# Keys and queries, values and local attention: sorted planes for LN1, and alternating column blocks

## The chip, the cores and the metric

The kernel runs on 1 core of a Trainium2 chip. The metric is the device time in microseconds (us), the median of the runs; lower is better. The core has TensorE (PE; its weight loads are shown apart as PEld), VectorE (DVE), ScalarE (ACT), GpSimd (POOL) and SyncE (SP, which only issues DMAs here). Everything is float32 apart from two constant matrices.

## The reference

Input `x` has shape (8, 32, 32, 32): 8 images, 32 channels, 32 x 32 pixels. Two layers follow each other.

```python
def layer0(x):                                  # 8 heads, d = 4 channels a head
    xn = ln_last(x, ln1_g, ln1_b)               # over the 32 columns of a row
    q, k, v = [conv(conv(xn, w1, 0), w3, 1).reshape(B, 8, H * W, 4) for w1, w3 in qkv]
    probs = softmax(einsum('bhpd,bhpe->bhde', k, q) / scale)
    attn = einsum('bhpd,bhde->bhpe', v, probs).transpose(0, 1, 3, 2).reshape(B, C, H, W)
    x = conv(attn, o_w, 0) + x
    xn = ln_last(x, ln2_g, ln2_b)
    return conv(gelu(conv(conv(xn, g1), g3)) * conv(conv(xn, i1), i3), r1) + x

def layer1(x):
    out = leaky_relu(instance_norm(conv(x, conv1_w, 1)))
    out1, mask = conv(out, conv2_w, 1), sigmoid(conv(out, mask_w, 1))
    xm = out * mask                             # q, k, v: 1x1 convolutions of xm
    out2 = attention of each pixel over its 3 x 3 neighbourhood
    return x + out1 * mask + (1 - mask) * out2
```

The reshape to (heads, H*W, 4) in `layer0` is of memory as it lies: a channel's image is cut into runs of 4 consecutive pixels, so the four entries of a head's vector are the columns x mod 4 = 0, 1, 2, 3 of one channel.

## The kernel before

The 8 images are worked in 4 pairs. A tensor of a pair stands as [128 partitions, 2 images, 256]: partition 32 r + c is channel c of row block r (8 rows of 32 pixels). For a 3 x 3 convolution the kernel builds shifted copies ("planes"): `sh_ln1` has 128 partitions, four blocks of 32 channels, and block s holds the whole image (34 rows with the padding) shifted by s - 1 columns, so that one matmul contracts over channels and columns at once and only the three rows dy are summed in PSUM. `shift_copies` (line 273) makes them out of `ln1_out`, cut by row blocks: DVE copies block 3 and block 0 (8 copies), ACT half of block 1 and block 2 (6 copies), and SP the other half of block 1 with two DMAs (`ln1_planes`, line 316). The same helper makes the planes of LN2, x2 and `act_c`; all DVE copies stand under line 278, all ACT copies under line 467.

Where the planes of LN1 are read:
- `qk` (line 1132): for each image, half, two column offsets d and three dy, one matmul with `sh_ln1` as stationary operand. Its 128 columns are 128 pixels with x mod 4 = d, taken with a step of 4 elements. The moving operand is the weight `w_qk`, 128 columns. 24 matmuls a pair.
- `v_by_head` (line 1143): 12 matmuls a pair, `w_v` (32 columns) stationary, the moving operand 512 pixels of the planes with a step of 4; output d goes to the PSUM partitions 32 d to 32 d + 31, which is column block d of the array.

`ln_apply` (lines 733 and 737) ends a layer norm: a product and a subtraction on DVE, 128 x 512 each. In local attention `window_scores` (line 1278) has, for each of two banks, 16 matmuls with a stationary operand of 64 columns, first 8 for column block 0 and then 8 for block 64; `window_out` (line 1302) has 32 matmuls with 32 stationary and 64 moving columns, 8 for each of four column blocks, block by block. A float32 matmul is two passes in the trace, so its counts are twice these.

The order on each engine is written out by hand, with semaphores between them. First comes the front of pairs 0 and 1, then a loop body `step(pair)`, run for pair 0 and (without the layer norm of a further pair) for pair 1, then a tail for pairs 2 and 3. In a body TensorE does the second layer of pair p, q/k and v of pair p + 2 between `conv1` and `mask_conv` of pair p, and the gate of pair p + 1 after the window scores. DVE's part for LN1 of pair p + 3 stands between `window_probs(p)` and `gated(p + 1)`. `average_mean` (line 1209) is a small matmul in the middle of `qk` that waits for DVE's statistics of `conv1`.

## Time and profile before

| | us |
|---|---|
| runs: median of 3 (lowest, highest) | 289.95 (288.15, 292.16) |
| profiled execution: span from its first to its last instruction | 286.2 |
| PE busy | 222.9 (78%) |
| PE weight loads busy | 143.5 (50%) |
| DVE busy | 189.8 (66%) |
| ACT busy | 129.2 (45%) |
| POOL busy | 75.9 (27%) |

The profiled execution is given by its span; some microseconds of a run lie outside it. Engines work side by side, so shares do not add up. Start and duration are in microseconds from the start of the span; "idle before" is the time for which an engine had nothing to do before a group, with the engine, tile and line that ended it. Names are those of the program with buffer numbers left out: `sh_ln` is `sh_ln1` or `sh_ln2`, `ln_out` is `ln1_out` or `ln2_out`.

### The profile page before, as it was taken

How to read it: one execution, taken by the hardware profiler on the slowest of the kernel's cores; microseconds unless marked ns; L12 is line 12 of the kernel's file. 1: busy time of each engine (PE TensorE's matmuls, PEld its weight loads, DVE VectorE, ACT ScalarE, POOL GpSimd, SP SyncE). 2: the span in 40 equal slices, each digit the busy share in tenths (PEclk: the TensorE clock that was granted, in tenths of full speed). 3: DMA queues.
4: the chain of work that ended last, by engine and by line, in shares of the span. 5: the costliest groups of instructions: out<-in, count | busy, mean ns of one | idle time of the engine just before them, and what ended most of it. 6: DMA issues, size and time to landing. Idle time of an engine off the chain costs nothing.

```text
span 286.2 us, 4575 instructions
## 1 busy us (share of the span) xinstructions
PE 222.9 (78%) x1738; PEld 143.5 (50%) x1738; DVE 189.8 (66%) x417; ACT 129.2 (45%) x256; POOL 75.9 (27%) x56
## 2 busy tenths in 40 slices
PE   0429868999669997798999986998529989368963
PEld 0229518824229734654589255745115536136843
DVE  5595365527596768999747974835999738882532
ACT  2230142234383355549822565429347557444440
POOL 3928204004004302540045125000464300304150
PEclk9999997999979999799999997999859999779987
DMA  7210011000011000000000200000000000000101
GB/s 198 53 46 2 0 40 53 0 2 0 1 55 37 2 0 1 2 0 21 0 2 0 73 3 1 2 0 2 0 37 3 0 0 3 0 0 3 39 0 39
DMA packets 3654, 5.17 MB, mean 18 GB/s; under 512 B 1136, under 2 KB 1872, under 8 KB 3632
## 3 DMA queue, kind: packets, MB, share of 16 engines
q1 hardware_dynamic: 3392, 4.29, 5.0%
q10 hardware_dynamic: 240, 0.58, 0.6%
q8 instruction: 14, 0.23, 0.3%
q14 instruction: 8, 0.07, 0.1%
HBM read 3.30 MB, written 1.05 MB: 15 GB/s over the span
## 4 chain that ended last, share of the span: by engine, by line
PE 64%; DVE 17%; ACT 10%; issue 5%; DMA 2%; SPq 0%; ACTq 0%; DVEq 0%
PE ps L1132 16%; PE ps L1186 15%; PE ps L1143 8%; PE ps L1278 6%; PE ps L1302 5%; PE ps L1222 4%; ACT sh_ln L467 4%; ACT p_t L560 3%; DVE sh_in L278 3%; DVE sh_ln L278 2%; DMA w3b<-in_w_gi 2%; PE ps L1262 2%; PE ps L1112 2%; DVE q_bd L933 1%; DVE xm L922 1%
## 5 line engine op out<-in xcount | busy, mean ns | idle before, releaser
L1132 PE MATMUL ps<-w_qk,sh_ln 128*128 128x128 f32 x192 | 46.9, 409 | 11.6 <-DVE sh_ln L278 7.8
L376 POOL TENSOR_TENSOR ln_s<-ln_s,neg_half 128x16 f32<-128x16 f32 x8 | 23.3, 2910 | 112.6 <-DVE ln_s L726 112.6
L1132 PEld LDWEIGHTS ps<-w_qk,sh_ln 128*128 128x128 f32 x192 | 45.6, 330 | 14.3 <-issue 14.3
L1186 PE MATMUL ps<-sh_ln,w_gi 96*128 96x512 f32 x96 | 42.4, 596 | 0.5 <-ACT v L484 0.5
L1222 PE MATMUL ps<-sh_in,w_in 128*32 128x256 f32 x384 | 25.6, 424 | 10.6 <-DVE sh_in L278 10.6
L467 ACT ACTIVATE sh_ln<-ln_out 32x496 f32<-32x496 f32 (+1 forms) x44 | 27.2, 618 | 11.6 <-DVE ln_out L737 11.0
L278 DVE COPY sh_ln<-ln_out 32x496 f32<-32x496 f32 (+2 forms) x60 | 28.0, 466 | 3.4 <-PE ps L1143 2.4
L1186 PEld LDWEIGHTS ps<-sh_ln,w_gi 96*128 96x128 f32 x96 | 17.9, 190 | 22.1 <-issue 21.9
L1222 PEld LDWEIGHTS ps<-sh_in,w_in 128*32 128x32 f32 x384 | 13.3, 123 | 23.3 <-DVE sh_in L278 10.8
L1143 PE MATMUL ps<-sh_ln,w_v 128*32 128x512 f32 x96 | 22.4, 1077 | 0.0
L829 DVE TENSOR_TENSOR gi<-ps,gate 64x512 f32<-64x512 f32 x16 | 11.1, 694 | 13.9 <-ACT gate L498 13.5
L479 ACT ACTIVATE qk_t<-ps 128x512 f32<-128x512 f32 x8 | 4.8, 597 | 34.0 <-PE ps L1132 34.0
L498 ACT ACTIVATE gate<-ps 64x512 f32<-64x512 f32 x16 | 9.4, 587 | 22.1 <-PE ps L1186 22.1
L1302 PE MATMUL ps<-p_t,v_t 128*32 128x64 f32 x256 | 14.2, 235 | 5.5 <-ACT p_t L560 5.5
L1278 PE MATMUL ps<-k_h,q_bd 128*64 128x60 f32 x256 | 17.8, 245 | 0.0
L1278 PEld LDWEIGHTS ps<-k_h,q_bd 128*64 128x64 f32 x256 | 16.6, 158 | 2.0 <-issue 2.0
L278 DVE COPY sh_in<-act_c 32x496 f32<-32x496 f32 (+1 forms) x28 | 17.2, 614 | 0.5
L1302 PEld LDWEIGHTS ps<-p_t,v_t 128*32 128x32 f32 x256 | 13.6, 120 | 7.7 <-issue 7.7
L1112 PE MATMUL ps<-sh_x,w_conv 128*32 128x512 f32 x96 | 12.4, 656 | 3.0 <-DVE sh_x L278 3.0
L467 ACT ACTIVATE sh_in<-act_c 32x496 f32<-32x496 f32 (+1 forms) x20 | 12.3, 617 | 4.9 <-DVE act_c L894 4.7
L400 POOL TENSOR_TENSOR omm<-ones,msk 128x512 f32<-128x512 f32 x4 | 6.6, 1648 | 28.2 <-DVE msk L912 28.0
L467 ACT ACTIVATE sh_x<-x 32x496 f32<-32x496 f32 (+1 forms) x20 | 12.3, 616 | 3.8 <-DVE x L836 3.6
(125 smaller groups left out, 336.5 us busy)
## 6 DMA issues: line engine op xcount, KB each, us to landing
x_norm<-in_x SPq DMA_DIRECT2D x4, 256.0 KB, 2.8
x_res<-in_x SPq DMA_DIRECT2D x4, 256.0 KB, 2.5
out_x<-out_s SPq DMA_DIRECT2D x4, 256.0 KB, 2.0
sh_ln<-ln_out SPq DMA_DIRECT2D x8, 64.0 KB, 2.0
kc<-in_shape_consts ACTq DMA_DIRECT2D x1, 450.0 KB, 5.8
w3b<-in_w_gi SPq DMA_DIRECT2D x1, 288.0 KB, 6.3
vec<-in_vectors SPq DMA_DIRECT2D x1, 131.5 KB, 3.3
w3a<-in_w_qkv ACTq DMA_DIRECT2D x1, 108.0 KB, 3.3
```

The lines of the kernel that those rows point to most:

```text
L278: ins = copy(plane(planes)[C * s:C * s + C, :, 1 + RH * r:1 + RH * r + RH, cut_left:cut_left + n], src[C * r:C * r + C, :, :].rearrange("p ...
L376: nc.gpsimd.tensor_tensor(ln_s[n][:, 3, :], ln_s[n][:, 2, :], neg_half[:, :], ALU.pow)\
L467: return nc.scalar.activation(o, i, ACT.Copy)
L498: nc.scalar.activation(gate[EC:P, n, :], ps[0:EC, GI_BANKS[n], :], ACT.Gelu).then_inc(g_gelu.sem, 1)
L829: nc.vector.tensor_tensor(gi[EC * (n % 2):EC * (n % 2) + EC, n // 2, :], ps[EC:P, GI_BANKS[n], :], gate[EC:P, n, :], ALU.mult).then_inc(g_ ...
L1112: mm = nc.tensor.matmul(ps[C * r:C * r + C, bank, :], weight(dy), plane(planes)[:, :, RH * r + dy:RH * r + dy + RH, 0:W], start=(dy == 0), ...
L1132: mm = nc.tensor.matmul(to, sh_ln1[:, i, at:at + D * P - D + 1:D], w_qk[:, dy, :, :, :].rearrange("p d m c -> p (d m c)"), start=(dy == 0) ...
L1143: mm = nc.tensor.matmul(ps[C * d:C * d + C, 2, :], w_v[:, dy, :], xs[:, :, dy:dy + H, d:d + W - D + 1:D], start=(dy == 0), stop=(dy == 2))
L1186: mm = nc.tensor.matmul(ps[:, GI_BANKS[2 * i + h], :], w_gi[:, dy, :, :].rearrange("p m o -> p (m o)"), xs[:, i, y:y + H // 2, 0:W], start ...
L1222: mm = nc.tensor.matmul(ps[C * r:C * r + C, bank, BLK * i:BLK * i + BLK], w_in[:, i, k, dy, :], plane(sh_in)[:, i, RH * r + dy:RH * r + dy ...
L1278: mm = nc.tensor.matmul(ps[C * r:C * r + 2 * C, 5 + bank, KEYS * n:KEYS * n + KEYS], q_bd[:, u, r:r + 2, :].rearrange("p r m -> p (r m)"), ...
L1302: mm = nc.tensor.matmul(o[:, i, a, b:b + 2, :, :], v_t[:, t, C * r:C * r + C], p_t[:, R * t + r, :, :].rearrange("p h m -> p (h m)"), star ...
```

## The change

`ln1_out` gets the form [128, 7 slots, 2 images, 8 rows x 8]. Slot 1 + d holds the pixels with x mod 4 = d; slot 0 holds those one column to the left of offset 0 (offset 3 of the neighbour at left), slots 5 and 6 those one and two to the right of offset 3. The final subtraction of LN1 writes slots 1 to 4 in that order, reading both operands with a step of 4; `ln1_neighbours`, two new DVE copies, fills slots 0, 5 and 6 from them (the edge stays zero, from a new memset at the start). Block s of `sh_ln1` is then slots s to s + 3 as they are, [4, 2 images, 34 rows x 8], and `slot_copies` takes the place of `shift_copies` for LN1, with the same number of copies on the same engines. `qk` and `v_by_head` read runs of consecutive elements. In `window_scores` and `window_out` the loops are exchanged, so that successive matmuls go to different column blocks. The matmuls and their number stay.

```diff
--- before.py
+++ after.py
@@ -61,6 +61,11 @@
 
 V_BC1, V_BC2, V_BM, V_BQ, V_BK, V_BV, V_SCALE, V_LN, V_OW = 0, 1, 2, 3, 4, 5, 6, 7, 7 + 4 * W
 V_END = V_OW + D * C
+WD = W // D
+SLOTS = D + 3
 
 
 
@@ -131,12 +136,12 @@
         x1 = sb("x1", [P, 2, BLK])
         x2 = sb("x2", [P, 2, BLK])
         out_s = sb("out_s", [P, 2, BLK])
-        ln1_out = sb("ln1_out", [P, 2, BLK])
+        ln1_out = sb("ln1_out", [P, SLOTS, 2, RH * WD])
         ln2_out = sb("ln2_out", [P, 2, BLK])
         act_c = sb("act_c", [P, 2, BLK])
         act_in = sb("act_in", [P, 2, BLK])
         w_in = sb("w_in", [P, 2, 2, 3, C])
-        sh_ln1 = sb("sh_ln1", [P, 2, PLANE])
+        sh_ln1 = sb("sh_ln1", [P, D, 2, (H + 2) * WD])
         sh_ln2 = sb("sh_ln2", [3 * C, 2, PLANE])
         sh_x2 = sb("sh_x2", [P, 2, PLANE])
         sh_in = sb("sh_in", [P, 2, PLANE])
@@ -184,7 +189,7 @@
 
         g_xn = signal("x_for_norm_loaded", 16)
         g_x = signal("x_for_sum_loaded", 16)
-        g_ln = [signal("ln1_steps", 7), signal("ln2_steps", 7)]
+        g_ln = [signal("ln1_steps", 9), signal("ln2_steps", 7)]
         g_sq = [signal("ln1_squares", 1), signal("ln2_squares", 1)]
         g_rs = [signal("ln1_rstd", 1), signal("ln2_rstd", 1)]
 
@@ -280,6 +285,19 @@
                            [:, :, :, cut_right:cut_right + n])
             return ins
 
+        def slot_planes(s, r):
+            at = (1 + RH * r) * WD
+            return sh_ln1[C * s:C * s + C, :, :, at:at + RH * WD].rearrange("p d i m -> p (d i) m")
+        def slots_of(s, r):
+            return ln1_out[C * r:C * r + C, s:s + D, :, :].rearrange("p d i m -> p (d i) m")
+        def slot_copies(copy, s, row_blocks):
+            for r in row_blocks:
+                ins = copy(slot_planes(s, r), slots_of(s, r))
+            return ins
 
         Z_LN1, Z_LN2, Z_X2, Z_IN, Z_PADS = 3, 4, 5, 6, 7
         W_QKV, W_ALL = 3, 8
@@ -312,9 +330,7 @@
                 sp.wait_ge(g_v4.sem, g_v4.before(pair))
                 sp.wait_ge(g_ln[0].sem, g_ln[0].done(pair))
                 for r in range(R // 2):
-                    start = (1 + RH * r) * W
-                    sp.dma_start(sh_ln1[C:2 * C, :, start:start + BLK], ln1_out[C * r:C * r + C])\
-                      .then_inc(planes_by["ln1"]["dma"].sem, 16)
+                    sp.dma_start(slot_planes(1, r), slots_of(1, r)).then_inc(planes_by["ln1"]["dma"].sem, 16)
 
             def store(pair):
                 alone(sp)
@@ -470,8 +486,12 @@
 
                 act.wait_ge(src_ready.sem, src_ready.done(pair))
                 act.wait_ge(reader.sem, reader.before(pair))
-                shift_copies(act_copy, src, dst, 1, range(R // 2, R) if name == "ln1" else (R - 1,))
-                shift_copies(act_copy, src, dst, 2, range(R)).then_inc(planes_by[name]["act"].sem, 1)
+                if name == "ln1":
+                    slot_copies(act_copy, 1, range(R // 2, R))
+                    slot_copies(act_copy, 2, range(R)).then_inc(planes_by[name]["act"].sem, 1)
+                else:
+                    shift_copies(act_copy, src, dst, 1, (R - 1,))
+                    shift_copies(act_copy, src, dst, 2, range(R)).then_inc(planes_by[name]["act"].sem, 1)
 
             def qk_t_evac(pair, i):
                 act.wait_ge(g_qkt.sem, g_qkt.at(pair, i + 1))
@@ -671,6 +691,7 @@
         def _(dve):
             for t in (w_bd, w_r1, w_conv, ps[:, 0, 0:12 * C], ps[:, 2, 0:3 * C]):
                 nc.vector.memset(t[:], 0.0).then_inc(s_zero_bd, 1)
+            nc.vector.memset(ln1_out[:, :, :, :], 0.0).then_inc(s_zero_bd, 1)
             dve.wait_ge(s_vec, 16)
 
             def folded_qkv():
@@ -734,8 +755,22 @@
                   .then_inc(g.sem, 1)
                 dve.wait_ge(g.sem, g.at(pair, 6))
                 planes_read(name, pair)
-                nc.vector.tensor_tensor(dst[:, :, :].rearrange("p i (y x) -> p (i y) x", x=W),
-                                        ln_per_col(2 * n + 1), ln_d[n][:, :, :], ALU.subtract).then_inc(g.sem, 1)
+                by_col, centered = ln_per_col(2 * n + 1), ln_d[n][:, :, :]
+                if n == 0:
+                    to = dst[:, 1:1 + D, :, :].rearrange("p d i (y x) -> p d (i y) x", x=WD)
+                    by_col, centered = [t.rearrange("p y (x d) -> p d y x", d=D) for t in (by_col, centered)]
+                else:
+                    to = dst[:, :, :].rearrange("p i (y x) -> p (i y) x", x=W)
+                nc.vector.tensor_tensor(to, by_col, centered, ALU.subtract).then_inc(g.sem, 1)
+            def ln1_neighbours(pair):
+                g = g_ln[0]
+                dve.wait_ge(g.sem, g.at(pair, 7))
+                rows = ln1_out[:, :, :, :].rearrange("p d i (y x) -> p d (i y) x", x=WD)
+                nc.vector.tensor_copy(rows[:, 0, :, 1:WD], rows[:, D, :, 0:WD - 1]).then_inc(g.sem, 1)
+                nc.vector.tensor_copy(rows[:, D + 1:SLOTS, :, 0:WD - 1], rows[:, 1:SLOTS - D, :, 1:WD])\
+                  .then_inc(g.sem, 1)
 
             def planes_read(name, pair):
 
@@ -748,10 +783,11 @@
                 dve.wait_ge(src_ready.sem, src_ready.done(pair))
                 dve.wait_ge(reader.sem, reader.before(pair))
                 if name == "ln1":
-                    shift_copies(nc.vector.tensor_copy, src, dst, 3, range(R))
+                    slot_copies(nc.vector.tensor_copy, 3, range(R))
+                    slot_copies(nc.vector.tensor_copy, 0, range(R)).then_inc(planes_by[name]["dve"].sem, 1)
                 else:
                     shift_copies(nc.vector.tensor_copy, src, dst, 1, range(R - 1))
-                shift_copies(nc.vector.tensor_copy, src, dst, 0, range(R)).then_inc(planes_by[name]["dve"].sem, 1)
+                    shift_copies(nc.vector.tensor_copy, src, dst, 0, range(R)).then_inc(planes_by[name]["dve"].sem, 1)
 
             def ln1_center(pair):
                 dve.wait_ge(g_xn.sem, g_xn.done(pair))
@@ -759,6 +795,7 @@
 
             def ln1_apply(pair):
                 ln_apply(0, ln1_out, "ln1", pair)
+                ln1_neighbours(pair)
                 planes("ln1", ln1_out, sh_ln1, g_ln[0], g_v4, pair)
 
             sm3 = [sm[:, k, :].rearrange("p (i e) -> p i e", e=D) for k in range(3)]
@@ -1017,6 +1054,7 @@
 
             ln1_center(0)
             ln_var(0, 0)
+            dve.wait_ge(s_zero_bd, 6)
             folded_qkv()
             dve.wait_ge(s_zero, Z_LN1)
             ln1_apply(0)
@@ -1025,6 +1063,7 @@
             other_constants()
             clear(ps[:, 4, :], ps[:, 7, :])
             ln_apply(0, ln1_out, "ln1", 1)
+            ln1_neighbours(1)
             head_scores(0)
             head_max(0)
             head_mix(0)
@@ -1128,8 +1167,8 @@
                         to = ps[:, i, 2 * P * h:2 * P * h + 2 * P]\
                             .rearrange("p (m d c) -> p d m c", m=2, d=D)[:, d:d + 2, :, :]
                         for dy in range(3):
-                            at = W * (H // 2 * h + dy) + d
-                            mm = nc.tensor.matmul(to, sh_ln1[:, i, at:at + D * P - D + 1:D],
+                            y = H // 2 * h + dy
+                            mm = nc.tensor.matmul(to, sh_ln1[:, d, i, WD * y:WD * y + P],
                                                   w_qk[:, dy, :, :, :].rearrange("p d m c -> p (d m c)"),
                                                   start=(dy == 0), stop=(dy == 2), skip_group_check=True)
                 if 1 in halves:
@@ -1137,11 +1176,10 @@
 
             def v_by_head(pair):
 
-                xs = plane(sh_ln1)
                 for dy in range(3):
                     for d in range(D):
                         mm = nc.tensor.matmul(ps[C * d:C * d + C, 2, :], w_v[:, dy, :],
-                                              xs[:, :, dy:dy + H, d:d + W - D + 1:D],
+                                              sh_ln1[:, d, :, WD * dy:WD * dy + WD * H],
                                               start=(dy == 0), stop=(dy == 2))
                 mm.then_inc(g_v4.sem, 1)
 
@@ -1271,10 +1309,10 @@
 
                     nc.tensor.matmul(ps[:, 5 + bank, 0:UPB * KEYS], ident_bf[:, :], win_bf[:, :],
                                      start=True, stop=False, skip_group_check=True)
-                    for r in range(0, R, 2):
-                        for n in range(UPB):
-                            u = UPB * bank + n
-                            i, a, b = u // (TA * TB), u // TB % TA, u % TB
+                    for n in range(UPB):
+                        u = UPB * bank + n
+                        i, a, b = u // (TA * TB), u // TB % TA, u % TB
+                        for r in range(0, R, 2):
                             mm = nc.tensor.matmul(ps[C * r:C * r + 2 * C, 5 + bank, KEYS * n:KEYS * n + KEYS],
                                                   q_bd[:, u, r:r + 2, :].rearrange("p r m -> p (r m)"),
                                                   k_h[:, i, TH * a:TH * a + KH, TW * b:TW * b + KW],
@@ -1295,10 +1333,10 @@
             def window_out(pair):
                 alone(pe)
                 pe.wait_ge(g_t_sb.sem, g_t_sb.done(pair))
-                for r in range(R):
-                    o = ps[C * r:C * r + C, 5, :].rearrange("p (i a y b x) -> p i a b y x", i=2, a=TA, b=TB, x=TW)
-                    for t in range(UNITS // 2):
-                        i, a, b = t // (TA * TB // 2), t // (TB // 2) % TA, 2 * (t % (TB // 2))
+                for t in range(UNITS // 2):
+                    i, a, b = t // (TA * TB // 2), t // (TB // 2) % TA, 2 * (t % (TB // 2))
+                    for r in range(R):
+                        o = ps[C * r:C * r + C, 5, :].rearrange("p (i a y b x) -> p i a b y x", i=2, a=TA, b=TB, x=TW)
                         mm = nc.tensor.matmul(o[:, i, a, b:b + 2, :, :], v_t[:, t, C * r:C * r + C],
                                               p_t[:, R * t + r, :, :].rearrange("p h m -> p (h m)"),
                                               start=True, stop=True)
```

On DVE the place is LN1 of pair p + 3 in the loop body, between the window softmax (`wsm`, `prob`) and the gating (`gi`), before:

```order
L967 TENSOR_TENSOR prob<-prob,wsm 128x8x60
L733 TENSOR_TENSOR ln_d<-ln_d,ln_s 128x512
L737 TENSOR_TENSOR ln_out<-vec,ln_d 128x512
L278 COPY sh_ln<-ln_out 32x2x8x30 x4
L278 COPY sh_ln<-ln_out 32x2x8x31 x4
L829 TENSOR_TENSOR gi<-ps,gate 64x512 x4
```

and now:

```order
L1004 TENSOR_TENSOR prob<-prob,wsm 128x8x60
L754 TENSOR_TENSOR ln_d<-ln_d,ln_s 128x512
L764 TENSOR_TENSOR ln_out<-vec,ln_d 128x512
L771 COPY ln_out<-ln_out 128x16x7
L772 COPY ln_out<-ln_out 128x32x7
L298 COPY sh_ln<-ln_out 32x8x64 x8
L866 TENSOR_TENSOR gi<-ps,gate 64x512 x4
```

Two copies stand between the subtraction and the eight copies to the planes, and the latter have runs of 64 elements where they had runs of 30 or 31.

On ACT it is the same place, between the first and second half of the gelu (`gate`), before:

```order
L498 ACT_TABLE_LOAD
L498 ACTIVATE gate<-ps 64x512 x2
L467 ACTIVATE sh_ln<-ln_out 32x2x256 x2
L467 ACTIVATE sh_ln<-ln_out 32x2x8x31 x4
L498 ACTIVATE gate<-ps 64x512 x2
```

and now:

```order
L518 ACT_TABLE_LOAD
L518 ACTIVATE gate<-ps 64x512 x2
L483 ACTIVATE sh_ln<-ln_out 32x8x64 x6
L518 ACTIVATE gate<-ps 64x512 x2
```

Nothing moved; six copies stay six, of 512 elements each. On SP the two DMAs of a pair have pieces of 64 elements instead of 256.

## Rows read from the trace of the kernel before

**Rows 1.** The page: span; busy us, share and instructions by engine.

```profile
span 286.2 us, 4575 instructions
PE 222.9 (78%) x1738; PEld 143.5 (50%) x1738; DVE 189.8 (66%) x417; ACT 129.2 (45%) x256; POOL 75.9 (27%) x56
```

**Rows 2.** The page: the chain that ended last, by line.

```profile
PE ps L1132 16%; PE ps L1186 15%; PE ps L1143 8%; PE ps L1278 6%; PE ps L1302 5%; PE ps L1222 4%; ACT sh_ln L467 4%; ACT p_t L560 3%; DVE sh_in L278 3%; DVE sh_ln L278 2%; DMA w3b<-in_w_gi 2%; PE ps L1262 2%; PE ps L1112 2%; DVE q_bd L933 1%; DVE xm L922 1%
```

**Rows 3.** Timeline, TensorE: start, duration, line, operation, tiles, shapes, count.

```profile
85.37 5.70 PEld L1132 LDWEIGHTS ps<-w_qk,sh_ln 128*128 128x128 f32 x24 [1.94 <-issue]
133.92 0.80 PEld L1289 LDWEIGHTS ps<-kc,prob 128*128 128x128 f32 x7 [0.29 <-issue]
...
98.66 5.59 PE L1143 MATMUL ps<-sh_ln,w_v 128*32 128x512 f32 x24
141.46 2.78 PE L1112 MATMUL ps<-sh_x,w_conv 128*32 128x512 f32 x24
```

**Rows 4.** Stretches: busy PE, PEld, DVE, ACT, POOL; granted clock; DMA.

```profile
45.40:48.70 3.30, 3.30 (x16) 3.30 (x16) 1.26 (x3) 0.36 (x1) 1.93 (x1) 0.50 0.11 42
...
175.20:178.40 3.20, 3.20 (x34) 3.09 (x33) 0.00 (x0) 1.10 (x8) 2.66 (x3) 0.50 0.00 0
```

**Rows 5.** Chain in order of time: start, duration, work.

```profile
235.30 1.82 PE ps L1278 x32
175.22 3.23 PE ps L1278 x32
257.58 3.15 PE ps L1302 x64
277.20 4.71 PE ps L1302 x64
```

**Rows 6.** Groups, 19.6 to 24.8, then 25 to 31: busy us, mean ns.

```profile
L1132 PE MATMUL ps<-w_qk,sh_ln 128*128 128x128 f32 x22 | 5.5, 445 | 7.8 <-DVE sh_ln L278 7.8
L1132 PE MATMUL ps<-w_qk,sh_ln 128*128 128x128 f32 x27 | 6.4, 396 | 0.0
```

**Rows 7.** Timeline, TensorE, values of local attention.

```profile
121.67 1.91 PE L1262 MATMUL ps<-w_bd,xw 128*60 128x128 f32 x30
```

**Rows 8.** Timeline, LN1 of pair 2 and the first `average_mean`.

```profile
81.49 3.77 ACT L467 ACTIVATE sh_ln<-ln_out 32x512 f32<-32x512 f32 x6 [1.32 <-DVE ln_out L737]
...
81.53 1.24 SPq L316 DMA_DIRECT2D sh_ln<-ln_out  x2
...
89.58 0.17 DVE L853 TENSOR_SCALAR inorm_v<-st 128x2 f32<-128x2 f32 x1
91.10 0.28 PE L1209 MATMUL ps<-st,kc 128*128 128x2 f32 x2
```

**Rows 9.** Groups, DVE: a reduction with a step, and one in order.

```profile
L805 DVE TENSOR_REDUCE mix_s<-mix_p 128x64 f32<-128x256 f32 x4 | 2.4, 598 | 0.1
...
L777 DVE TENSOR_REDUCE sc_d<-sc_m 128x8 f32<-128x256 f32 x4 | 1.7, 420 | 0.1
```

**Rows 10.** Timeline, LN1 of pair 0 beside POOL's last memset.

```profile
12.57 6.79 DVE L278 COPY sh_ln<-ln_out 32x480 f32<-32x480 f32 x8
...
14.25 1.91 POOL L370 MEMSET sh_in<- 128x2176 f32 x1
```

**Rows 11.** Timeline, DVE, LN1 of pair 3 and the gating.

```profile
129.56 3.34 DVE L278 COPY sh_ln<-ln_out 32x480 f32<-32x480 f32 x8
...
132.93 2.87 DVE L829 TENSOR_TENSOR gi<-ps,gate 64x512 f32<-64x512 f32 x4
```

**Rows 12.** DMA issues: tiles, queue, count, KB each, median us to landing.

```profile
sh_ln<-ln_out SPq DMA_DIRECT2D x8, 64.0 KB, 2.0
...
w_bd<-in_l_qkv SPq DMA_DIRECT2D x4, 12.0 KB, 3.5
```

**Rows 13.** Timeline, ACT's planes of LN2, DVE's of `act_c`.

```profile
104.93 3.13 ACT L467 ACTIVATE sh_ln<-ln_out 32x512 f32<-32x512 f32 x5
...
154.09 5.40 DVE L278 COPY sh_in<-act_c 32x512 f32<-32x512 f32 x7
```

## The prediction, made before the changed kernel had run

> **What bounds the kernel now.** I read the page's engine shares first: PE is busy 78% of a span of 286.2 us [rows 1]. Then the chain that ended last: its largest lines are PE's L1132 (q/k, 16%), L1186 (15%) and L1143 (v, 8%); L1278 (window scores) and L1302 (window output) have 6% and 5% [rows 2]. So TensorE sets most of the end, and the change touches four of these five lines. Next the timeline, for what one instruction costs. A float32 matmul stands in the trace as two passes, each a weight load (PEld) and a MATMUL. In q/k the 24 weight loads of one image take 5.70 us, 0.238 each, back to back: the stationary operand is `sh_ln1` read at every fourth element. The transposes L1289 load as many columns from consecutive elements, 7 in 0.80 us, 0.114 each. In v the moving operand is strided: 24 passes take 5.59 us, while L1112, with the same shapes (128x32 stationary, 512 columns) and rows read in order, takes 2.78 [rows 3]. Both strided reads cost twice the contiguous one, on either operand, and this is the sentence on which most of the forecast rests.
>
> **Part 1, q/k.** 48 passes a pair, each 0.238 -> 0.114: 5.9 us a pair, 23.7 for the four. Bounds: nothing (if the loads are slow for another reason) and 23.7. Here the clock comes in. While loads took 0.238 a lower clock was hidden: from 45.4 to 48.7 the granted clock was 0.50 (1.2 GHz) and q/k kept its pace, 16 passes in 3.3 us with those that overlap the ends [rows 4]. Once a pass is short the matmul shows it: 32 score passes take 3.23 us at half clock and 1.82 at full [rows 4, 5], a factor 1.77, so a q/k pass costs 0.20 there. The second pair has 3.4 us of it (loss 1.5 us). For the first pair the view of the clock shows nothing of the kind, but its MATMULs average 445 ns up to 24.8 and 396 after [rows 6]; I take the first 5.2 us to be at half clock too: 26 passes where full clock would give 46, a loss of 2.3. Part 1 is 23.7 - 3.8 = 19.9.
>
> **Part 2, v.** 5.59 - 2.78 = 2.8 a pair, 11.2 in all.
>
> **Part 3, alternating column blocks.** How much two blocks overlap is seen in L1262, where successive matmuls already alternate between two: 30 passes with 128 moving columns in 1.91 us, 0.064 each [rows 7], against 0.114 in L1289 [rows 3]. So I halve the scores: a bank's 32 passes 1.82 -> 0.95. For window output (four blocks, 64 passes, 3.15 us [rows 5]) the ends are nothing and a quarter (0.8); I take 1.8, since no row shows weight loads this close together with so few moving columns, and two blocks are the nearest. At half clock, the last one, 4.71 us [rows 5] also goes to about 1.8.
>
> **Part 4, what is added.** On DVE a memset of 896 elements, before `vec` lands, where DVE has nothing: nothing. Per pair: two neighbour copies of 112 and 224 elements, and the subtraction at the old L737 reads both operands and writes at a step. The copies: 0.2 and 0.3 us, between the row of a copy of about 500 elements (3.34/8 = 0.42, [rows 11]) and nothing. The subtraction: a reduction of 256 elements takes 0.60 us with a step and 0.42 in order [rows 9]; twice that difference for 512 is 0.35. Together 0.9 us, ends 0.3 and 1.5. (The Trainium skill, SBUF — State Buffer, Specifications, gives SBUF lines of 16 bytes and wants two hits on each for full bandwidth; a step of four floats gives one. By that rule the subtraction would double, to 1.4 us instead of 1.04, and the sum lose about 1 us more, 261; the reductions of [rows 9] show a factor of 1.4, the matmuls one of 2.) The slot copies are as many and as long as the shift copies: nothing. All copies to `sh_ln1` (DVE 8, ACT 6, two DMAs) now wait for the neighbours.
> - Pair 0: DVE's first shift copy is held until POOL's memset ends at 16.16 (8 copies take 6.79 us), while ACT and the DMAs ran beside it [rows 10]. The neighbour copies will be held there instead, and ACT's six copies (3.77) start only behind them, at about 16.6: q/k starts 0.9 us later.
> - Pair 2: PE waits for ACT's copies in 81.49 to 85.27 [rows 8]: 0.9 later.
> - Pair 3: the planes are done long before their use. But DVE runs without a pause there until the gating [rows 11]: 0.9 later on `gi`, less 0.5 because the second score bank no longer keeps DVE waiting.
> - DMA pieces shrink from 1024 to 256 bytes. Issued at 81.53, the second one lands 1.24 + 2.0 = 3.2 us later, ACT takes 3.77 [rows 8, 12]. The nearest row for small pieces is `w_bd` (128 bytes, from HBM) at 3.5 us: then the planes are 1.0 late in three pairs. I take 0, with 3 us as the other end.
>
> **Where gains get lost.** In iteration 0 DVE's statistics are ready at 89.75; PE asks at 91.1 [rows 8]. PE will ask 2.9 us sooner than before relative to its start, DVE 0.9 later than ACT's copies allow: 1.5 us of waiting. After v, ACT copies ln2's planes (3.13 us) before it can do the tanh [rows 13]; ACT now gets ahead of DVE's `ln2_out`, 1.1 us lost. In iteration 1 DVE's seven `in` copies take 5.40 us, since POOL's final operations hold them [rows 13]; before, q/k and v covered them; now they end 1.2 after v, and ln2's planes behind them hold the tanh 1.6 longer. Small hand-offs around v4: 0.2.
>
> **Sum.** 19.9 + 11.2 = 31.1. Less 0.9, 0.9, 1.5, 1.1, 2.8, 0.2: 23.7. Pair 0's second half +0.5 (scores 0.5, output 0.9, DVE -0.9), pair 1: scores 1.3, output 1.1. That makes 26.6. Pair 2's scores lie beside DVE's copies of x2 (0.2), its output is on the chain (1.3); pair 3's scores give 1.4, its output 2.9: 5.8. Total 32.4. Shorter bursts leave PE more pauses, and half clock came only after pauses; a stretch of 3.4 us does 1.9 us' worth of work, so costs 1.5 where PE is the bound. I allow one and a half new ones, 2.4. Gain 30.0. The profiled span is 286.2; the median of the runs is 289.95, so 3.7 us lie outside it and stay: 286.2 - 30.0 + 3.7 = **260.0 us**.
>
> **Rivals.**
> - A, the hand-offs or the clock eat more (0.16): four new half-clock stretches (6 us), or DVE and ACT the bound after each q/k, so that a third of Part 1 is lost: 265 to 272. For: PE's waits are already on DVE and ACT. Against: PE's own lines stand on top of the chain [rows 2].
> - B, the weight loads are not slow for their step (0.07): the output of q/k is written in runs of 32 floats, and w_qk may matter. Then the 19.9 of Part 1 is gone, and with it some 3 of the lost hand-offs and 2 of the clock: 32.4 - 19.9 + 3 = 15.5, about 275. Against: v shows the same factor.
> - C, the DMA copies end last (0.04 by itself): q/k of three pairs starts up to 1 us later, 263. The Trainium skill (DMA: Bandwidth & Descriptors, Specifications) wants at least 512 bytes for line rate and so speaks against 256-byte pieces; the same page calls slow small descriptors a matter of HBM only. By the first the time would be that 263.
> - D, better (0.08): window output at a quarter (1.0 less three times) and no new half clock (2.4): 254.6 or a little less.
> - E, slower (0.02): TensorE sinks to 1.2 GHz for good. Each 3.4 us stretch costs 1.5, so it decides from 21 new stretches on (32.4 / 1.5), 71 us more at half clock; if all of the 150 us of PE that remain on the chain ran there, x 1.77, it would be some 375 us. Against: the scores that took 3.23 at 175 take 1.82 at 235 [rows 5], so it comes back.
> - F, hardly any change (0.03): behind PE's savings DVE and ACT set each iteration, and only the 5.8 us of the last two pairs arrive: 284. Against: in iteration 1 nothing but PE separates the start of q/k from the end of v, save the copies named.
>
> **Range and chances.** The forecast (254 to 265) has 0.60. To hold 8 in 10 I take in half of A and of D, C, and the ends of Part 4: 253 to 269. A measurement of this kernel tells about 2%, 5.8 us, from no change. Faster by over that: forecast, A, B, C, D, 0.95. Within: F, 0.03. Slower: E, 0.02.
>
> **What would show it.** L1132's successor: 48 loads a pair near 0.114, half-clock stretches excepted. v: 24 passes in about 2.8. Scores 32 passes near 1 us at full clock, output 64 near 1.8. The subtraction near 1.0 us, neighbours 0.2 and 0.3. The mean matmul (average) of iteration 0 waits for DVE's statistics. What would make it wrong: q/k loads still above 0.2; PE waiting for `sh_ln1` by a DMA; a PE clock at 0.5 in most slices; PE idle after v longer than 3 us an iteration.

## The result, and the profile after the change

The changed kernel takes 258.5 us (median of four runs, 254.9 to 260.7) against 289.7 for the kernel before on the same chip: a ratio of 0.885, 95% interval 0.879 to 0.892. The forecast was 260.0, range 253 to 269. A second measurement (e9 below) gave 258.5 again and a ratio of 0.894 (0.889 to 0.898), so two measurements of one kernel differ by about 1%, and smaller differences between the experiments below are told as such. Every ratio and its interval leave out runs more than 1.5% above the fastest of their kernel (the slow ones), while the medians hold all runs.

The page of the changed kernel, first busy time by engine, then the chain by engine and by line. These answer [rows 1, 2].

```profile
span 256.4 us, 4585 instructions
PE 182.8 (71%) x1738; PEld 111.0 (43%) x1738; DVE 192.4 (75%) x426; ACT 129.3 (50%) x256; POOL 76.1 (30%) x56
...
DVE 43%; PE 36%; ACT 8%; issue 7%; DMA 3%; POOL 1%; SPq 1%; ACTq 0%; DVEq 0%
PE ps L1224 12%; DVE sh_in L283 6%; PE ps L1171 5%; PE ps L1260 5%; DVE sh_ln L298 3%; DVE sh_ln L283 3%; DMA w3b<-in_w_gi 3%; ACT sh_x L483 2%; PE ps L1151 2%; DVE ln_out L764 2%; PE ps L1232 2%; DVE sh_x L283 2%; PE ps L1316 2%; PE ps L1300 2%; DVE gi L866 2%
```

TensorE lost 40 us of busy time and DVE gained 2.6. q/k (old L1132, now L1171) fell from 16% of the chain to 5%; v (old L1143, now L1181), with 8% before, is not among its lines any more. DVE, with 43% of the chain, now sets more of the end than TensorE. The next matmul to look at is not one of these any more, it is the gate/info convolution, L1224.

The four groups that the change is about. Each row: line, engine, operation, tiles, shapes, count, busy us, mean ns of one, idle time before. Before, the same groups stood at 46.9 (L1132), 22.4 (L1143), 17.8 (L1278) and 14.2 us (L1302).

```profile
L1171 PE MATMUL ps<-w_qk,sh_ln 128*128 128x128 f32 x192 | 26.6, 302 | 12.8 <-ACT sh_ln L483 12.8
L1181 PE MATMUL ps<-sh_ln,w_v 128*32 128x512 f32 x96 | 11.1, 596 | 0.0
L1316 PE MATMUL ps<-k_h,q_bd 128*64 128x60 f32 x256 | 10.8, 246 | 0.0
L1340 PE MATMUL ps<-p_t,v_t 128*32 128x64 f32 x256 | 6.9, 290 | 5.1 <-ACT p_t L580 5.1
```

And the price of one pass, from the timeline of TensorE and its weight loads (start, duration, line, operation, tiles, shapes, count). These answer [rows 3] and [rows 5].

```profile
77.92 1.42 PEld L1171 LDWEIGHTS ps<-w_qk,sh_ln 128*128 128x128 f32 x12
82.42 2.78 PE L1181 MATMUL ps<-sh_ln,w_v 128*32 128x512 f32 x24
151.29 1.97 PE L1316 MATMUL ps<-k_h,q_bd 128*64 128x60 f32 x32
210.18 1.15 PE L1316 MATMUL ps<-k_h,q_bd 128*64 128x60 f32 x32
171.99 1.10 PE L1340 MATMUL ps<-p_t,v_t 128*32 128x64 f32 x64 [0.76 <-ACT p_t L580]
232.66 1.94 PE L1340 MATMUL ps<-p_t,v_t 128*32 128x64 f32 x64 [2.25 <-ACT p_t L580]
```

Twelve loads of q/k take 1.42 us, 0.118 each; v's 24 passes 2.78. Scores and window output have two prices each: at full clock 1.15 and 1.10 us, at half clock 1.97 and 1.94. The granted clock of the stretches says which is which (busy time of PE, PEld, DVE, ACT, POOL; granted clock; DMA):

```profile
147.10:157.10 10.00, 8.78 (x86) 6.39 (x88) 6.05 (x13) 4.88 (x21) 3.78 (x3) 0.50 0.01 2
...
232.40:235.60 3.20, 2.94 (x69) 2.81 (x70) 0.17 (x1) 0.80 (x2) 0.18 (x1) 0.50 0.02 5
```

### The profile page after: what moved, and what is told of

The parts are those of the page before. It is cut to its first block, busy times and chain, and to the rows that moved or that the text cites. A ratio compares the mean times of both kernels' runs of the same rounds, so it can differ in the third digit from the quotient of the medians.

```text
span 256.4 us, 4585 instructions
## 1 busy us (share of the span) xinstructions
PE 182.8 (71%) x1738; PEld 111.0 (43%) x1738; DVE 192.4 (75%) x426; ACT 129.3 (50%) x256; POOL 76.1 (30%) x56
## 4 chain that ended last, share of the span: by engine, by line
DVE 43%; PE 36%; ACT 8%; issue 7%; DMA 3%; POOL 1%; SPq 1%; ACTq 0%; DVEq 0%
PE ps L1224 12%; DVE sh_in L283 6%; PE ps L1171 5%; PE ps L1260 5%; DVE sh_ln L298 3%; DVE sh_ln L283 3%; DMA w3b<-in_w_gi 3%; ACT sh_x L483 2%; PE ps L1151 2%; DVE ln_out L764 2%; PE ps L1232 2%; DVE sh_x L283 2%; PE ps L1316 2%; PE ps L1300 2%; DVE gi L866 2%
## 5 line engine op out<-in xcount | busy, mean ns | idle before, releaser
L1224 PE MATMUL ps<-sh_ln,w_gi 96*128 96x512 f32 x96 | 42.4, 596 | 0.5 <-DVE sm L822 0.5
L483 ACT ACTIVATE sh_ln<-ln_out 32x512 f32<-32x512 f32 (+1 forms) x44 | 27.4, 622 | 22.0 <-DVE ln_out L772 15.3
L1171 PE MATMUL ps<-w_qk,sh_ln 128*128 128x128 f32 x192 | 26.6, 302 | 12.8 <-ACT sh_ln L483 12.8
L1260 PE MATMUL ps<-sh_in,w_in 128*32 128x256 f32 x384 | 26.2, 432 | 11.4 <-DVE sh_in L283 11.4
L1171 PEld LDWEIGHTS ps<-w_qk,sh_ln 128*128 128x128 f32 x192 | 25.4, 216 | 16.4 <-issue 16.4
L1224 PEld LDWEIGHTS ps<-sh_ln,w_gi 96*128 96x128 f32 x96 | 17.9, 190 | 22.1 <-issue 21.9
L866 DVE TENSOR_TENSOR gi<-ps,gate 64x512 f32<-64x512 f32 x16 | 11.1, 694 | 15.0 <-ACT gate L518 14.7
L518 ACT ACTIVATE gate<-ps 64x512 f32<-64x512 f32 x16 | 9.3, 587 | 20.2 <-PE ps L1224 20.2
L1151 PE MATMUL ps<-sh_x,w_conv 128*32 128x512 f32 x96 | 12.7, 664 | 5.7 <-DVE sh_x L283 4.4
L298 DVE COPY sh_ln<-ln_out 32x512 f32<-32x512 f32 x32 | 13.4, 418 | 0.5
L283 DVE COPY sh_x<-x 32x496 f32<-32x496 f32 (+1 forms) x28 | 11.5, 411 | 0.5
L283 DVE COPY sh_ln<-ln_out 32x496 f32<-32x496 f32 (+1 forms) x28 | 11.5, 411 | 0.5
L1181 PE MATMUL ps<-sh_ln,w_v 128*32 128x512 f32 x96 | 11.1, 596 | 0.0
L1316 PE MATMUL ps<-k_h,q_bd 128*64 128x60 f32 x256 | 10.8, 246 | 0.0
L398 POOL TENSOR_TENSOR inorm_v<-inorm_v,neg_half 128x2 f32<-128x2 f32 x4 | 4.3, 1076 | 21.9 <-DVE inorm_v L924 21.9
```

What stands on the lines that cost most here:

```text
L283: ins = copy(plane(planes)[C * s:C * s + C, :, 1 + RH * r:1 + RH * r + RH, cut_left:cut_left + n], src[C * r:C * r + C, :, :].rearrange("p ...
L298: ins = copy(slot_planes(s, r), slots_of(s, r))
L483: return nc.scalar.activation(o, i, ACT.Copy)
L518: nc.scalar.activation(gate[EC:P, n, :], ps[0:EC, GI_BANKS[n], :], ACT.Gelu).then_inc(g_gelu.sem, 1)
L866: nc.vector.tensor_tensor(gi[EC * (n % 2):EC * (n % 2) + EC, n // 2, :], ps[EC:P, GI_BANKS[n], :], gate[EC:P, n, :], ALU.mult).then_inc(g_ ...
L1151: mm = nc.tensor.matmul(ps[C * r:C * r + C, bank, :], weight(dy), plane(planes)[:, :, RH * r + dy:RH * r + dy + RH, 0:W], start=(dy == 0), ...
```

## The experiments

The experiments ran on three chips, each beside its own runs of the kernel before: 289.5 us beside e1 to e4, 288.1 beside e5 to e8, 289.1 beside e9 to e12.

**e1 and e2, one half each.** e1 is the kernel before with only the loops of scores and window output exchanged; e2 is the changed kernel with only those loops put back.

```diff
-                    for r in range(0, R, 2):
-                        for n in range(UPB):
-                            u = UPB * bank + n
-                            i, a, b = u // (TA * TB), u // TB % TA, u % TB
+                    for n in range(UPB):
+                        u = UPB * bank + n
+                        i, a, b = u // (TA * TB), u // TB % TA, u % TB
+                        for r in range(0, R, 2):
...
```

> The kernel before with the exchanged loops of window scores and window output alone; the planes of LN1 stay as they were. The theory of the prediction: the score lines fall from 17.8 us of busy time to about 11 and the output from 14.2 to about 7, and on the chain this gives some 9 us (5.8 of them in the last two pairs): about 281 us, ratio 0.97. Rival (the two halves of the change only pay together, or shorter bursts bring more half clock): under 4 us, ratio above 0.985.

> The changed kernel with the loops of window scores and window output in their old order; sorted planes, neighbour copies and reads in order stay. The theory of the prediction: the other 21 to 23 us, about 267 us, ratio 0.925; q/k 26 to 27 us busy, v about 11. If the two halves are worth less together than apart, this kernel and the one with the loops alone gain more than 31 us between them.

e1 took 279.9 us, ratio 0.966 (0.956 to 0.975), e2 266.7, ratio 0.913 (0.904 to 0.923). The gains, 9.6 and 22.8, add up to 32.4 of the whole's 31: the two halves of the change do not help or hinder each other by more than the runs can tell. In e1 the window output of pair 0 (and below it that of pair 2) shows the price of four alternating blocks without the other half:

```profile
137.11 1.10 PE L1302 MATMUL ps<-p_t,v_t 128*32 128x64 f32 x64 [0.58 <-ACT p_t L560]
...
255.55 1.93 PE L1302 MATMUL ps<-p_t,v_t 128*32 128x64 f32 x64 [2.24 <-ACT p_t L560]
```

3.15 became 1.10 at full clock. The output of pair 2 at 255.55 ran at half clock, where the kernel before had full clock for it [rows 5], and so kept only 1.2 of 2.05 us. What e1 changes is the order as a whole: no run changes it and keeps successive matmuls in one block. That the alternation is what pays rests on that order and on the older lines that alternate already [rows 7].

**e3 and e4, is it the step?** e3 is the kernel before, in which each q/k weight load reads 128 consecutive elements of the old plane instead of every fourth (so q and k come from other pixels, as many of them). e4 reads every second element, in q/k and in v (other pixels too).

First the edit of e3, then that of e4.

```diff
-                            mm = nc.tensor.matmul(to, sh_ln1[:, i, at:at + D * P - D + 1:D],
+                            mm = nc.tensor.matmul(to, sh_ln1[:, i, W * (H // 2 * h + dy) + d:W * (H // 2 * h + dy) + d + P],
```

```diff
-                            mm = nc.tensor.matmul(to, sh_ln1[:, i, at:at + D * P - D + 1:D],
+                            mm = nc.tensor.matmul(to, sh_ln1[:, i, at:at + 2 * P - 1:2],
...
-                                              xs[:, :, dy:dy + H, d:d + W - D + 1:D],
+                                              xs[:, :, dy:dy + H, d:d + 15:2],
```

> The kernel before, with only the q/k matmuls reading 128 consecutive elements of the planes instead of every fourth (other pixels, so q and k are not those of the reference); no new copies, v stays strided. Theory (the step makes the weight loads slow): q/k weight loads fall from 45.6 us busy to about 25, and the time by about 16 to 18 us, to 272. Rival B of the prediction (q/k is slow for its scattered output or its moving operand): loads stay near 45 us and the time near 289.

> The kernel before, with q/k and v reading every second element instead of every fourth (other pixels, so q, k and v are not those of the reference). The rule of the Trainium skill (SBUF — State Buffer, Specifications), two hits for each 16-byte line, gives two floats of each line at a step of two: q/k passes at 0.11 us and v's 24 passes in 2.8 us, as if in order. Rival (any step other than one halves the rate): 0.235 and 5.6 as before.

e3 took 271.8 us, ratio 0.943 (0.934 to 0.952), e4 265.7 in its one run. Twelve q/k loads in the kernel before, in e4 and in e3:

```profile
91.21 2.89 PEld L1132 LDWEIGHTS ps<-w_qk,sh_ln 128*128 128x128 f32 x12
```

```profile
79.04 1.50 PEld L1132 LDWEIGHTS ps<-w_qk,sh_ln 128*128 128x128 f32 x12
```

```profile
81.38 1.42 PEld L1132 LDWEIGHTS ps<-w_qk,sh_ln 128*128 128x128 f32 x12
```

0.241 a pass at a step of four floats, 0.125 at two, 0.118 in order. The output is written in the same runs of 32 floats in all three, and `w_qk` is read alike, so rival B, that the loads are slow for something else, falls. And the cost is not "strided or not": a step of two floats costs 6% on the stationary operand. On the moving one it costs more: v's MATMULs take 14.9 us in all in e4, between the 22.4 at a step of four and the 11.1 in order. One pair of it, with the clock at full:

```profile
29.96 3.71 PE L1143 MATMUL ps<-sh_ln,w_v 128*32 128x512 f32 x24
```

The Trainium skill (SBUF — State Buffer, Specifications) wants two hits on each 16-byte line for full bandwidth; a step of two floats gives two hits, a step of four one. The stationary operand follows that within 6%. v at step two is 34% above the row in order, but its reads differ from those in more than the step. They come in runs of 8 elements, a run for each image row, and the runs of d = 2 and 3 start in the middle of a line, so they touch five lines for eight elements and two of the five only once. The single passes in the trace of e4 fall into two kinds, half of them 0.65 us long and half 0.76, where every pass in order takes 0.59. The first two column blocks to start, those of d = 0 and 1 in the kernel's order, have the short ones. So the step itself seems to cost v about 10%, and where its runs start the rest; no run separates the two, and this stays argued.

**e5, the neighbour slots left out.** The changed kernel without the two copies (so slots 0, D + 1 and D + 2 of `ln1_out` stay zero, and the convolution reads zeros there for neighbouring columns; the count of LN1's signals goes from 9 to 7 with them): what do they cost with the wait behind POOL's memset?

```diff
-                nc.vector.tensor_copy(rows[:, 0, :, 1:WD], rows[:, D, :, 0:WD - 1]).then_inc(g.sem, 1)
-                nc.vector.tensor_copy(rows[:, D + 1:SLOTS, :, 0:WD - 1], rows[:, 1:SLOTS - D, :, 1:WD])\
-                  .then_inc(g.sem, 1)
```

> The changed kernel without the two neighbour copies on DVE (slots 0, 5 and 6 keep zeros, so the planes lack their neighbours). By the trace of after, the copies cost 0.5 us a pair where nothing holds them, on the chain in three pairs, and in pair 0 they are held by POOL's memsets until 16.3 while ACT's six copies wait behind them: DVE's own eight copies are held as long, so pair 0 gains only about 0.8. In all 2 to 2.5 us, ratio to the kernel before about 0.877 instead of 0.885. If the copies were worth more than 4 us, the price in Part 4 of the prediction was too low.

255.2 us, ratio 0.885 (0.881 to 0.889), against 0.885 and 0.894 for the changed kernel: between nothing and 1%. The 2 to 2.5 us expected are thus neither shown nor ruled out. The start of pair 0's q/k moves only from 20.41 to 20.00, because the next copies are held in their place:

```profile
13.70 6.01 DVE L298 COPY sh_ln<-ln_out 32x512 f32<-32x512 f32 x8
```

Eight copies that take 3.44 elsewhere take 6.01. So it is not the neighbours that are dear at the start, it is the memset beside them (e6 shows that: without it the neighbours take 0.22 and 0.27 us and the eight copies 3.44).

**e6, POOL's clears behind the second square root.**

```diff
-            clear(sh_ln2)
-            clear(sh_x2)
-            clear(sh_in)
             rstd(0, 1)
+            clear(sh_ln2)
+            clear(sh_x2)
+            clear(sh_in)
```

> The changed kernel with POOL clearing the planes of LN2, x2 and the activation after the second rstd instead of before it. Theory (what holds DVE's copies at 13.4 to 16.4 is POOL's memset, not the data): the neighbour copies take 0.5 us, q/k of pair 0 starts near 17.6 instead of 20.4, and 2.5 to 3 us arrive at the end, about 255.5. Rival: the moved memsets then hold DVE's later copies of pairs 0 and 1, and nothing is gained.

261.4 us, ratio 0.906 (0.903 to 0.910): worse. q/k of pair 0 starts at 17.25, three us earlier, as the theory said. But the clears now stand beside the neighbour copies of pair 1 (first row, DVE), and v of pair 0, queued behind DVE's scores, starts at 33.15 instead of 30.53 and runs at half clock (PE):

```profile
24.66 6.95 DVE L771 COPY ln_out<-ln_out 128x112 f32<-128x112 f32 x1
```

```profile
33.15 5.34 PE L1181 MATMUL ps<-sh_ln,w_v 128*32 128x512 f32 x24
```

A copy of 112 elements, 0.22 us by itself, lasted 6.95 and over the ends of five of POOL's seven memsets; it ended as the last one, of `p_t`, began at 31.49. Three us won at the start were paid for with a hold of seven.

**e7 and e8, filling TensorE's pauses.** In e7 eight matmuls without a use stand ahead of the scores (into a bank that is free there) and four ahead of `reduce_1`; e8 is e6 and e7 together.

```diff
+            def filler(bank, n):
+                for _ in range(n):
+                    nc.tensor.matmul(ps[:, bank, 0:UPB * KEYS], ident_bf[:, :], win_bf[:, :],
+                                     start=True, stop=True, skip_group_check=True)
...
                 window_k(pair)
+                filler(0, 8)
                 window_scores(pair)
...
                 probs_transposed(pair)
+                filler(6, 4)
                 reduce_1(pair + 1)
```

> The changed kernel with matmuls whose results nobody reads in two pauses of TensorE in the loop: 8 of 480 bfloat16 columns ahead of the window scores and 4 ahead of the r1 matmuls. Theory (the pause before the scores brings the stretch of half clock over scores and window v in iteration 1): that stretch goes, the scores' two banks take 1.0 instead of 1.9 us and window v 1.9 instead of 2.6, so 2 to 3 us are gained, and the granted clock rises from 0.90. Rival: the stretches come from low load over a longer time and stay; the fillers then cost up to 1 us.

> The later clears and the filler matmuls together. If both work and lie in different places, their gains add: about 253 us, 5 us under the changed kernel.

e7: 257.7 us, ratio 0.897 (0.892 to 0.903); e8: 261.6, ratio 0.908 (0.903 to 0.913). In e7 the stretch from 147.1 to 157.1, at half clock in the changed kernel, is at full clock (first fence, same columns as above), and the gate/info convolution behind it starts at 155.67 instead of 158.18. But the first convolution of pair 1, 2.78 us in the changed kernel, now meets the half clock (second row of the first fence, and the PE row of the second):

```profile
147.10:157.10 10.00, 8.95 (x114) 6.03 (x115) 7.64 (x18) 6.87 (x24) 3.78 (x3) 1.00 0.01 2
122.40:125.60 3.20, 3.20 (x16) 0.79 (x20) 3.05 (x5) 2.54 (x4) 0.00 (x0) 0.50 0.02 5
```

```profile
122.32 4.42 PE L1151 MATMUL ps<-sh_x,w_conv 128*32 128x512 f32 x24 [1.94 <-DVE sh_x L283]
```

1.6 us are lost there, and at the next q/k e7 is 0.3 behind (126.67 for 126.33); at gate/info it is 2.5 ahead. So the 10 us at half clock had cost 2.8, not the 4.5 that my 1.5 for each 3.4 us gives: TensorE is idle for 1.2 of them anyway. The span of the profiled execution is 1.1 us shorter, the ratio no better. Yet over the whole execution TensorE spent 37 us at half clock instead of 51 (2 x 0.073 x 255.3 us, at a mean granted clock of 0.927, against 2 x 0.100 x 256.4). So 14 us less at half clock shortened the span by 1.1 us, the fillers' own time included. e8 missed its 253 us: it kept e6's loss.

**e9 to e12, a version that avoids e6's fault.** e9 is the changed kernel again, as the reference. e10 puts POOL's clears into gaps and writes the neighbour slots with a two-source operation. e11 is e10 with the one-source copies kept. e12 is e10 with the filler ahead of the scores only. The edit of e10 against the changed kernel:

```diff
             rstd(0, 0)
+            rstd(0, 1)
             clear(sh_ln2)
             clear(sh_x2)
             clear(sh_in)
-            rstd(0, 1)
             clear(xm)
+            rstd(1, 0)
+            rstd(0, 2)
             clear(q_bd, s_late)
             clear(prob, s_late)
             clear(p_t, s_late)
-            rstd(1, 0)
-            rstd(0, 2)
...
-            dve.wait_ge(s_late, 5)
             gated(0, 0)
...
             ln1_apply(2)
+            dve.wait_ge(s_late, 5)
             with dve.Fori(0, PAIRS - 3) as pair:
...
-                nc.vector.tensor_copy(rows[:, 0, :, 1:WD], rows[:, D, :, 0:WD - 1]).then_inc(g.sem, 1)
-                nc.vector.tensor_copy(rows[:, D + 1:SLOTS, :, 0:WD - 1], rows[:, 1:SLOTS - D, :, 1:WD])\
-                  .then_inc(g.sem, 1)
+                for to, x in ((rows[:, 0, :, 1:WD], rows[:, D, :, 0:WD - 1]),
+                              (rows[:, D + 1:SLOTS, :, 0:WD - 1], rows[:, 1:SLOTS - D, :, 1:WD])):
+                    nc.vector.tensor_tensor(to, x, x, ALU.max).then_inc(g.sem, 1)
```

> The changed kernel itself once more, as the reference for the three runs beside it on the same chip. 258.5 us as before, within 1.5 us, and about 0.89 of the kernel before. If it comes out further off, the comparisons of the earlier experiments with it, which were made on other chips, are uncertain by as much.

> Three edits of the start: POOL's clears of the other planes and xm stand behind the second square root, its clears of the window buffers behind the square root of pair 2, and the two copies of the neighbour slots are a maximum of a tensor with itself, which has two sources. Theory (POOL's memset holds one-source copies of DVE and lets two-source operations run): the neighbour slots of pair 1 take 0.2 and 0.3 us beside the memset, where e6 had 6.95, q/k of pair 0 starts at 17.3 us instead of 20.4, planes of pair 1 are at most 1 us late, and 2 to 3 of those 3 us last: 256 us. Rival (DVE is held by POOL's memset whatever the operation is): the maximum is held to the end of the clears, about 29 us, v of pair 0 ends about 2.5 us later than in the changed kernel: 260 us or more. Second rival (what is gained at the start is eaten by another pattern of half-clock stretches): starts moved earlier as in the theory, and the time within 1 us of the changed kernel's.

> The same as e10_start, with the neighbour slots written by one-source copies as in the changed kernel. Theory (one-source copies are held): the copies of pair 1 that start at about 24.7 us end with the memset of xm at about 29 us, 4.3 us after their start, and v of pair 0 ends about 4 us later than in e10_start; 259 us. Rival (length of the hold in e6 had another cause than the kind of operation): same as e10_start.

> e10_start with the eight filler matmuls ahead of the scores of each pair, as in e7, and none ahead of reduce_1. Theory (a pause of TensorE ahead of the scores brings the half clock on scores, v windows and gate/info): the scores of pair 1 take 2.9 us instead of 4.9 wherever they had fallen to half clock, about 1 to 2 us less in the span than e10_start: 254.5 us. Rival (the half clock is only moved to another place, as conv1 of pair 1 showed in e7): within 1 us of e10_start.

| kernel | us, median | ratio, interval |
|---|---|---|
| e9, the changed kernel | 258.5 | 0.894 (0.889 to 0.898) |
| e10 | 256.1 | 0.879 (0.872 to 0.885) |
| e11 | 257.2 | 0.888 (0.883 to 0.893) |
| e12 | 256.6 | 0.886 (0.880 to 0.892) |

e10's ratio goes by its two faster runs, 253.3 and 254.8 us; the other two took 257.3 (the profiled one) and 258.0. All four are below e9's four, 258.2 to 259.0.

The neighbours of pair 1 in e10 (two operations in 0.58 us) and in e11 (3.71 us, to the end of POOL's memset of `sh_in`):

```profile
25.44 0.58 DVE L773 TENSOR_TENSOR ln_out<-ln_out 128x112 f32<-128x112 f32 x2
```

```profile
25.32 3.71 DVE L771 COPY ln_out<-ln_out 128x112 f32<-128x112 f32 x1
...
27.05 1.90 POOL L386 MEMSET sh_in<- 128x2176 f32 x1
```

In both kernels POOL runs the same memsets, from 23.5 to 29.7 us. This shows it: POOL's memset holds DVE's one-source copies and lets its two-source operations run. The Trainium skill (SBUF — State Buffer, SBUF: two separate sides) has the rule: GpSimd and a DVE operation in a two-port mode lock each other out for a whole instruction, and a DVE operation with two SBUF inputs only meets a GpSimd operation that reads SBUF, which a memset does not. The rows agree on both counts; that the hold can outlast a memset and go on through the next ones (one boundary in e11, five in e6) is what the rows add.

What comes of the earlier start: e10 starts q/k at 18.04, where the changed kernel starts it at 20.41 in its first trace and at 20.63 in that of e9. But e10 ends it at 26.42, the changed kernel at 27.78 and, in e9, at 28.61. The loads per 2 us (busy time and count of PEld, granted clock, DMA) show why. For e10, then the first trace of the changed kernel:

```profile
18.00:20.00 2.00, 2.00 (x10) 1.00 0.02 7
...
22.00:24.00 2.00, 2.00 (x11) 1.00 0.00 0
24.00:26.00 2.00, 2.00 (x19) 1.00 0.06 12
```

```profile
20.50:22.50 2.00, 2.00 (x11) 1.00 0.00 0
22.50:24.50 2.00, 2.00 (x13) 1.00 0.00 0
24.50:26.50 2.00, 2.00 (x19) 1.00 0.04 8
```

And for e11, whose q/k starts at 17.91, and for e9:

```profile
20.00:22.00 2.00, 2.00 (x15) 1.00 0.00 0
22.00:24.00 2.00, 2.00 (x20) 1.00 0.03 8
```

```profile
24.50:26.50 2.00, 2.00 (x15) 1.00 0.00 0
26.50:28.50 2.00, 2.00 (x20) 1.00 0.05 12
```

In all of them the loads first come at 0.21 us each. That is the pace of a recorded half clock: from 37.8 to 41.2 in the changed kernel, at 0.50, a q/k load takes 0.213 too. The slow pace ends at 21.0 us in e11, 24.0 in e10, 24.1 in the changed kernel and 25.7 in e9, which is the same kernel. The 1.00 in these rows is no measurement: the trace's own record of the clock begins with an entry of full clock at just these times (21.0, 23.9, 24.1, 25.6), and the view counts time without an entry as full. So the first stretch of q/k ran at half clock, as the prediction took it to; where it ends differs by 1.5 us between two executions of one kernel, and an earlier start can mean more work at the slow pace.

How much of the start lasts can be read against two traces of the changed kernel, and they differ. Against the first, the 1.35 us that e10 is ahead at the first convolution of pair 0 (66.05 for 67.40) are gone at the first `average_mean`, 77.56 for 77.70: q/k of pair 2 meets half clock from 71.8 to 78.4 and takes 5.46 instead of 2.92. The last output starts at 249.48 for 250.08, so 0.6 of 2.4 us last. Against e9, on the same chip, q/k of pair 2 takes 5.46 in both, and e10 is 2.2 ahead at the first convolution (68.22), 2.0 at `average_mean` (79.55) and 1.7 at the last output (251.22): 1.7 of 2.6 us last. And e11, 3.6 us behind e10 at the first convolution of pair 0, is only 0.6 behind at the last output, since it has no half clock from 123.4 to 181.4 while e10 has one of 6.8 us. So the half-clock stretches, which lie differently even in two executions of one kernel, move single spans by as much as the start does. Over four runs each the medians of e9 and e10 differ by 2.4 us, and the intervals of the ratios do not touch. The second rival of e10 is thus half right. e12's interval overlaps e10's: filling brings nothing here, as in e7. e10 is 0.9% (by medians) to 1.7% (by ratios) ahead of the changed kernel on its own chip, and not clear of e11 and e12, whose intervals overlap its own.

## Why the prediction was right, step by step

Gains at marks of the timeline (the start of a stage unless said) against what the sum had reached there, ahead of its 2.4 for new half-clock stretches:

| mark | before | after | gain | sum |
|---|---|---|---|---|
| q/k of pair 0 ends | 31.11 | 27.78 | 3.3 | 5.9 - 2.3 - 0.9 = 2.7 |
| gate/info, pair 0 | 63.24 | 50.37 | 12.9 | 11.8 - 3.8 + 5.6 - 0.9 = 12.7 |
| window q, pair 0 | 110.11 | 91.54 | 18.6 | + 8.7 - 0.9 - 1.5 - 1.1 = 17.9 |
| first convolution, pair 1 | 141.46 | 123.62 | 17.8 | + 0.5 = 18.4 |
| window q, pair 1 | 168.91 | 144.84 | 24.1 | + 8.7 - 2.8 = 24.3 |
| first convolution, pair 2 | 200.24 | 175.24 | 25.0 | + 2.4 = 26.7 |
| last output ends | 281.90 | 252.01 | 29.9 | + 5.8 = 32.5, less 2.4 = 30.1 |

- **Part 1, q/k.** Expected 0.238 -> 0.114, measured 0.241 -> 0.118; PEld busy fell by 20.2 us (45.6 to 25.4), expected 19.9. e3 shows the cause. The first pair lost less to the slow pace than I took (48 loads in 7.4 us, expected 5.5 + 2.3 = 7.8), but that is the luck of one execution: in e9, the same kernel, they took 8.0.
- **Part 2, v.** Expected 5.59 -> 2.78, measured 2.78.
- **Part 3, alternating blocks.** Two terms were off, one each way. Scores: expected 0.95 a bank, measured 1.10 in the chain, so 0.72 saved instead of 0.87. Window output: I took two blocks' worth, 1.8; at full clock it is 1.10, 2.9 times as fast as before, nearer to the quarter that rival D had. The number nevertheless came out, since three of the four outputs ran at half clock (1.94, 1.94 and 1.93), which I had not foreseen. That is luck of the sum, and no merit of the step.
- **Part 4, what is added.** L764 takes 1.08 to 1.13 us for LN1, where it took 0.7: +0.42 on the mean, expected 0.35 (a doubling would have been 0.7). The neighbours take 0.22 and 0.27 when nothing holds them, as expected. In pair 0 they are held to the end of the memset, as foreseen. The chain in order of time:

```profile
12.19 1.09 DVE ln_out L764
13.44 2.93 DVE ln_out L772
16.45 0.63 ACT sh_ln L483
...
20.41 7.38 PE ps L1171 x48
```

  q/k starts 0.8 us later than before (0.9 expected). The DMA pieces of 256 bytes land in 2.1 us instead of 2.0, so rival C falls. The memset of `ln1_out` costs nothing.
- **Where gains get lost.** The first `average_mean` waits for DVE's statistics as foreseen, 1.34 us for an expected 1.5:

```profile
77.70 0.38 PE L1247 MATMUL ps<-st,kc 128*128 128x2 f32 x2 [1.34 <-DVE st L887]
```

  In iteration 1 it does not wait, and DVE's seven `in` copies and ACT's planes behind them eat the rest: 6.2 us gained between the first convolution and window q, expected 5.9.
- **Clock, the step that was mis-sized.** Mean granted clock fell from 0.937 to 0.900. At half clock 0.5 is missing, so the time there is twice the missing share: 2 x 0.063 x 286.2 = 36 us before, 2 x 0.100 x 256.4 = 51 after: four and a half new stretches of 3.4 us where I allowed one and a half. (Both means leave out the start, where the clock has no entry.) By stage, three of them lie in the loop: one more around the scores and the output of pair 0, two more on the scores of pair 1, where 175.1 to 178.5 became 147.1 to 157.1. One lies on the output of pair 2, and the rest behind the end of the last output, 252.01, where it costs nothing. The two stretches in which TensorE waits most for DVE are not new. They stood in the kernel before too, as long and with the same waits; first before, then after (PE first):

```profile
205.80:216.00 10.20, 3.62 (x34) 1.93 (x38) 9.79 (x19) 4.67 (x8) 6.26 (x6) 0.50 0.07 26
246.80:253.60 6.80, 4.05 (x40) 1.98 (x44) 6.56 (x14) 2.40 (x4) 1.16 (x2) 0.50 0.00 0
```

```profile
181.20:191.30 10.10, 3.80 (x37) 1.78 (x40) 9.82 (x18) 5.38 (x9) 5.43 (x6) 0.50 0.07 26
222.20:228.80 6.60, 4.43 (x44) 2.14 (x48) 6.38 (x15) 1.83 (x3) 0.58 (x1) 0.50 0.00 0
```

  In the table the sum runs 1.7 us too high up to the first convolution of pair 2, with three new stretches, and 0.9 behind it, with one: 2.6 for an allowance of 2.4, in which the two wrong terms of Part 3 sit as well. So a price of 1.5 each was too dear: four of them would have been 6. e7 points the same way, with 2.8 us for the stretch that is three long. Count and price were both wrong, and nearly cancel; that is luck too.

- **Outside the span.** I set the median, 289.95, against the profiled span, 286.2, and kept 3.7 us. They are of different executions. Of one and the same, 1.5 lie outside (257.9 for a span of 256.4). The span forecast was 256.2 and came out at 256.4; with 1.5 it would have been 257.7 us, and the median is 258.5.
- **Rivals.** B falls by e3, C by the landing time, E and F by the result. A was right that four or more half-clock stretches come, wrong that they cost 6 us. D was right about the window output at full clock.
